# Four transformer layers on one core: VectorE makes the softmax levels of the quantised layer, and its feed-forward is laid over three phases

## The reference

```python
def _fq(x, delta, zp, n_bits):
    xi = _round_ste(x / delta) + zp
    xq = jnp.clip(xi, 0.0, 2.0 ** n_bits - 1.0)
    return (xq - zp) * delta

def _attn(x, ctx, wq, wk, wv, wo, bo, dq, dk, dv, dw):
    ...
    sim = jnp.einsum('bhid,bhjd->bhij', _fq(q, dq, 128.0, 8), _fq(k, dk, 128.0, 8)) * SCALE
    attn = jax.nn.softmax(sim, axis=-1)
    out = jnp.einsum('bhij,bhjd->bhid', _fq(attn, dw, 0.0, 8), _fq(v, dv, 128.0, 8))
    ...
h1 = _ln(x, ln1_g, ln1_b)
x = _attn(h1, h1, a1_wq, ...) + x
h2 = _ln(x, ln2_g, ln2_b)
x = _attn(h2, context, a2_wq, ...) + x
h3 = _ln(x, ln3_g, ln3_b)
hg = h3 @ ff_w1 + ff_b1
a, g = jnp.split(hg, 2, axis=-1)
x = a * jax.nn.gelu(g, approximate=False) @ ff_w2 + ff_b2 + x
```

## Time and profile before

| | us |
|---|---|
| median of 3 runs (range) | 2011.68 (2011.1 to 2012.37) |
| the profiled execution | 2007.97 |
| its span in the trace | 2006.2 |
| layer 1, from the first score of its first phase to the end of its last full phase | 631.76 |
| PE / DVE / ACT / POOL busy in the whole span | 1808.6 / 1237.6 / 1074.7 / 905.3 |
| PE / DVE / ACT / POOL busy in those 631.76 | 553.14 / 337.72 / 386.03 / 311.02 |

### The profile page before, as it was taken

The page is one execution under the profiler, slowest core; times in us unless marked ns, Lnnn a source line. Parts: engine busy times, 40 slices in busy tenths (PEclk is TensorE's granted clock), DMA queues, the critical chain, the costliest instruction groups (busy, mean ns, idle before and its releaser), DMA issues.

```text
span 2006.2 us, 34807 instructions
## 1 busy us (share of the span) xinstructions
PE 1808.6 (90%) x12481; PEld 1344.1 (67%) x12481; DVE 1237.6 (62%) x2220; ACT 1074.7 (54%) x3142; POOL 905.3 (45%) x1209
## 2 busy tenths in 40 slices
PE   4998988789799889889999999999999999999997
PEld 4887876466566656657667677676676676766766
DVE  5899995744654464463575665865746647365471
ACT  2232225665575475565575564655645656565662
POOL 4466554654463363363254443644444333333340
PEclk8999998788878878879999999999999999999999
DMA  7200000002000000000002000000000000000000
GB/s 226 92 11 6 11 6 6 1 7 90 1 6 6 1 6 6 0 6 7 1 7 90 1 7 6 7 7 1 7 6 2 12 1 7 22 7 1 12 1 11
DMA packets 31073, 35.66 MB, mean 18 GB/s; under 512 B 3164, under 2 KB 29752, under 8 KB 30520
## 3 DMA queue, kind: packets, MB, share of 16 engines
q1 hardware_dynamic: 30904, 33.44, 5.2%
HBM read 31.34 MB, written 2.10 MB: 17 GB/s over the span
## 4 chain that ended last, share of the span: by engine, by line
PE 61%; DVE 17%; ACT 10%; issue 6%; POOL 2%; SPq 2%; DMA 1%; DVEq 0%; POOLq 0%; ACTq 0%
PE ps L594 33%; PE ps L806 6%; PE ps L744 6%; PE ps L816 5%; PE ps L850 4%; ACT work L983 3%; ACT work L990 3%; DVE work L1183 3%; DVE xn L1037 2%; PE ps L607 2%; DVE rowmax L1187 2%; PE ps L831 2%; ACT hT L899 1%; PE ps L766 1%; POOL work L1376 1%
## 5 line engine op out<-in xcount | busy, mean ns | idle before, releaser
L594 PE MATMUL ps<-hT,w_slot 128*128 128x256 f32 x1696 | 410.1, 396 | 17.1 <-ACT hT L899 16.1
L1300 POOL TENSOR_TENSOR work<-KT,own_head 128x512 f32<-128x512 f32 x256 | 262.4, 1046 | 285.4 <-PE ps L806 179.9
L594 PEld LDWEIGHTS ps<-hT,w_slot 128*128 128x128 f32 x1696 | 323.5, 196 | 77.2 <-ACT hT L899 21.7
L990 ACT ACTIVATE work<-work,rowmax 128x128 f32<-128x128 f32 x768 | 244.9, 391 | 167.8 <-DVE rowmax L1187 167.0
L816 PEld LDWEIGHTS ps<-ident,work 128*128 128x128 f32 x1536 | 200.1, 153 | 170.0 <-issue 90.4
L983 ACT ACTIVATE work<-ps,rowmax,score_scale 128x128 f32<-128x128 f32 x512 | 229.3, 484 | 118.7 <-DVE rowmax L1191 118.3
L816 PE MATMUL ps<-ident,work 128*128 128x128 f32 x1536 | 266.4, 302 | 17.9 <-ACT work L990 17.0
L806 PE MATMUL ps<-work,QT 128*128 128x512 f32 x512 | 266.4, 605 | 10.0 <-POOL work L1300 4.9
L1376 POOL TENSOR_SCALAR work<-work,winv 128x128 f32<-128x128 f32 x512 | 185.0, 382 | 167.7 <-DVE winv L1203 165.3
L1217 DVE RECIPROCAL O<-ps 128x128 f32<-128x128 f32 x128 | 122.3, 955 | 174.6 <-PE ps L850 173.9
L976 ACT ACTIVATE work<-ps 128x512 f32<-128x512 f32 x256 | 150.7, 596 | 91.4 <-PE ps L816 91.2
(11 more groups left out here) (131 smaller groups left out, 3170.3 us busy)
## 6 DMA issues: line engine op xcount, KB each, us to landing
ctx_in<-in_ctx SPq DMA_DIRECT2D x32, 256.0 KB, 2.7
w_slot<-in_L_xattn_W SPq DMA_DIRECT2D x2, 1024.0 KB, 6.2
w_slot<-in_L_xattn_ff_w SPq DMA_DIRECT2D x1, 2048.0 KB, 11.5
w_slot<-in_L_xattn_ffn_w SPq DMA_DIRECT2D x2, 1024.0 KB, 9.8
w_slot<-in_L_xattn_w SPq DMA_DIRECT2D x2, 1024.0 KB, 10.0
out<-x_all SPq DMA_DIRECT2D x8, 256.0 KB, 2.1
x_all<-in_x SPq DMA_DIRECT2D x1, 1536.0 KB, 11.4
pad<-in_mask_Bx1x1xS_fk SPq DMA_DIRECT2D x1, 1024.0 KB, 7.6
```

The source lines that it names most:

```text
L594: mm = pe.matmul(dst, lhsT(k), rhs(k), start=(k == 0 and not onto), stop=(k == chunks - 1 and not more))
L990: ex = act.activation(prob[i % NPF][:, tok(h)], src[:, tok(h)], ACT.Exp, bias=shifts[:, at:at + 1])
L1300: pool.tensor_tensor(KB[u % NK].rearrange("p (h k) -> p h k", h=HU), keys, own_head[:, e:HC:2].unsqueeze(2).broadcast_to([P, HU, S]), ALU. ...
```

## The change

Two things are changed in layer 1, and the order of its pieces.

1. **Levels.** ScalarE's line 974 and the constants `top` and `below` are gone. VectorE takes a turned unit out of PSUM with the smaller of x and MAGIC + 255, minus MAGIC: the level itself. Its place in VectorE's queue is behind the row maximum and the inverses of the same step. Line 831 multiplies only the levels, four matmuls for a unit, and the output scale loses its minus sign.
2. **Order.** For the groups 0 to 2 the feed-forward of a stream is cut in three: four `f` in steps 8 to 11 of one phase, four in steps 8 to 11 of the next, and `y2` in four parts in steps 0 to 3 of the one after that. Stream 0 has its first four `f` in C, its last four in D and its `y2` in the next A; stream 1 has them in the next A, B and C. So every one of these phases carries four `f`, and A and C also a `y2`. The chain that ends in `k`, `q`, `v` of the next group goes along in C and D. Group 3, which leads into layer 2, keeps `joined` for its own feed-forward.
3. **Banks.** In these phases the feed-forward has bank `one` alone: every `f` writes it, and waits until VectorE has read the one before. `ctx`, `tin`, `k`, `q`, `v` and `y` share `other`; so `q` waits for `k_ready` and `v` for `q_ready`.

```diff
+SPREAD_START = {"tin": 3, "ctx": 4, "bias": 4, "k": 7, "q": 8, "v": 9, "keys": 9}
+SPREAD_NORM = {"norm": 8, "scale": 10}
+SPREAD_HIDDEN = 8
+SPREAD_SUM = 4
...
+    hidden = [(SPREAD_HIDDEN + int(piece[1:]) % (FC // 2), piece, arg, n) for piece, _, arg, n in pieces[:y2] if piece[0] == "f"]
+    product = [(part, f"y2{part}", pieces[y2][2], pieces[y2][3]) for part in range(Y2)]
...
+                attend(layer, g, 1, 0, middle(0) + into_a)
...
+                attend(layer, g, 0, 1, middle(1) + start(0, SPREAD_NORM) + into_b)
+                chain_0, first_0, second_0, product_0 = end(0)
+                attend(layer, g, 1, 1, chain_0 + start(0, SPREAD_START) + first_0 + start(1, SPREAD_NORM) + into_c)
+                chain_1, first_1, second_1, product_1 = end(1)
+                attend(*after, 0, 0, chain_1 + start(1, SPREAD_START) + second_0)
+                return product_0 + first_1, second_1, product_1
...
+                            pe.wait_ge(q["k_ready" if piece == "q" else "q_ready"], C * (use("att", layer, g, n["att"]) + 1))
...
+                            pe.wait_ge(q["hid_ready"], FC * use("ffn", layer, g, n["ffn"]) + f)
+                        product(one[:, 0:T], lambda k: w1[:, k, FF + f * P:FF + (f + 1) * P], lambda k: hT[st][:, k, :], C)
...
-                            rhs = below[:, :].broadcast_to([P, S]) if n < 2 else PTb[u % 2][:, tok(2 * x + e)]
...
-                            act.activation(PTb[u % 2], bank(2 + u % 2), ACT.Relu, bias=top[:, 0:1], scale=-1.0).then_inc(s["PT_ready"], 1)
...
+                def levels(u):
+                    dve.wait_ge(s["o_ps"], U * ap + u + 1 - 2)
+                    dve.wait_ge(s["PT_ps"], U * ap + u + 1)
+                    dve.tensor_scalar(PTb[u % 2], bank(2 + u % 2), MAGIC + 255.0, MAGIC, ALU.min, ALU.subtract).then_inc(s["PT_ready"], 1)
```

More of the change, by code:

```diff
@@ L172, with spread_closing @@
 FIRST_AHEAD = 2
+SPREAD = 1
+MIDDLE_SHIFT = {"yadd": -1}
+SPREAD_START = {"tin": 3, "ctx": 4, "bias": 4, "k": 7, "q": 8, "v": 9, "keys": 9}
+SPREAD_NORM = {"norm": 8, "scale": 10}
+SPREAD_CLOSING = {"ot": 0, "y": 1, "sum": 1, "norm": 2, "scale": 4, "tin": 6, "bias": 8}
+SPREAD_HIDDEN = 8
+SPREAD_SUM = 4
+def spread_closing(layer):
+    pieces = PLAN[layer][-1]
+    y2 = [piece for piece, _, _, _ in pieces].index("y2")
+    chain = [(SPREAD_CLOSING[piece], piece, arg, n) for piece, _, arg, n in pieces[:y2] if piece[0] != "f"]
+    hidden = [(SPREAD_HIDDEN + int(piece[1:]) % (FC // 2), piece, arg, n) for piece, _, arg, n in pieces[:y2] if piece[0] == "f"]
+    product = [(part, f"y2{part}", pieces[y2][2], pieces[y2][3]) for part in range(Y2)]
+    product.append((SPREAD_SUM,) + pieces[y2 + 1][0:1] + pieces[y2 + 1][2:])
+    return chain, hidden[:FC // 2], hidden[FC // 2:], product
 CLOSING_SLOT = {"ot": 0, "y": 1, "sum": 1, "norm": 2, "scale": 3, "post": 5, "tin": 7, "bias": 8}
@@ L476, in passes @@
             left = []
[L477 to L481, removed]
+            for g in range(NG - 1):
+                left = joined_pass(0, g, (0, g + 1), left)
+            before_last(0)
+            left = joined_pass(0, NG - 1, (1, 0), left), [], []
+            for g in range(NG - 1):
+                left = spread_pass(SPREAD, g, (SPREAD, g + 1), left)
+            before_last(SPREAD)
+            left = spread_pass(SPREAD, NG - 1, (SPREAD + 1, 0), left)
             for layer in range(FIRST_AHEAD, NL):
@@ L882, in emit @@
                         act.wait_ge(q["ctx_ps"], use("ctx", layer, g, 0) + 1)
-                        act.activation(cT[st].rearrange("p c t -> p (c t)"), one, ACT.Copy).then_inc(q["ctx_ready"], 1)
+                        act.activation(cT[st].rearrange("p c t -> p (c t)"), other if spread else one, ACT.Copy).then_inc(q["ctx_ready"], 1)
                     elif piece == "stage":
@@ L896, in emit @@
                         act.wait_ge(q["tin_ps"], due("tin", layer, g, n["tin"]) + 1)
+                        target = hT_ahead[st] if ahead and not (spread and n["att"] == PER_PASS["att"][layer]) else hT[st]
                         for m in range(C):
@@ L934, in emit @@
                         k = use("ffn", layer, g, n["ffn"])
-                        b = one if f % 2 == 0 else other
+                        b = one if spread or f % 2 == 0 else other
                         if arg["act"] == "geglu":
@@ L1013, in emit @@
                 def emit(piece, arg, n):
+                    spread = ahead == "spread"
                     swapped = ahead or "early" in arg
@@ L1018, in emit @@
                         if n["yadd"]:
-                            dve.wait_ge(q["yadd_done"], G * use("yadd", layer, g, n["yadd"]))
+                            dve.wait_ge(q["yadd_done"], G * due("yadd", layer, g, n["yadd"]))
                         else:
@@ L1225, in step @@
                         inverses((i - SUM_LAG) // 2)
+                    if quant and 0 <= i - lag < U:
+                        levels(i - lag)
                     u = i - lag - 1
```

90 lines of the change are left out of this document (71 added, 19 removed).

## The result

The changed kernel takes 2030.38 us (median of 4 runs, 2028.32 to 2030.99), the kernel before 2011.39 beside it: a ratio of 1.0099, 95% interval 1.0085 to 1.0113. The forecast was 1975, with 2024 as the upper end. It is slower, and outside the range. Times are medians; one run of e12 took 6116.01 us, and is in that kernel's median but not in its ratio.

The account below looks back on a forecast made before the run. TensorE, 90% busy, has an idle first half in A and B and a packed second in C and D; evening out takes a group from 160.6 to 149.6. Summed over the layer, 2011.68 - 36.9 = 1975 us; range 1938 to 2024.

Parts of the forecast that it names:

- The phases that keep their order ... lose `below` only.: First phase, A and B of group 0, C of group 3: -0.7 us each, -2.8 in all.
- I let it return in the same place: TensorE's clock returns to full within a few us of the start of `k`, as before the change.
- rival 2: Clock stays low in second halves: +8.9 us a phase, range 2020 to 2082, value 2040; chance 0.12.
- The Trainium skill's rule: Short idles between groups of matmuls make the clock go up and down; speaks against the change, toward the second rival's sum.
- First half with `y2`: A and C up to `k`: 19.0 us, 2.5 more than 16.5, for 7.07 of `y2` work.
- `tin` and `ctx`, 0.7 us: Two more transposed pieces in C and D push ScalarE: C 39.0 against A 38.3, D 36.5 against B 35.8.
- Levels, a gain of 0.5 in the first half: Levels take 0.75 us on VectorE; without the product with `below`, first half goes from 17.0 to 16.5.
- Quantising 1.8 and 2.25: Second half of a spread phase: VectorE needs 1.8 us for quantised `k`, 2.25 each for `q` and `v`.
- rival 3: VectorE's queue becomes the bound: 4.25 us by 12 phases, +51, 2026; chance 0.12.
- The second half, 15.9: Spread phase from `k`'s end to next first score: 15.9 us, TensorE waiting 1.85; a phase B had 7.9.
- The sum over the layer: Layer 1: D -46.7, C -35.8, A and B +45.9, last `y2` +2.5, phases keeping order -2.8: -36.9 us.
- make the 8.0: Second half's growth from 7.9 to 15.9: four `f` 7.1, waits 1.85, 0.7 less for `below`.

Follow-up runs that it names:

- e12: The kernel before with the four transposes of units 0 to 3 issued twice in each phase: 1998.17 us, ratio 0.9944.
- e3: The changed kernel with `q` in the feed-forward's idle bank again in phases A and B of group 0: 2016.36 us, ratio 1.0025.
- e5: The changed kernel with the four transposes of units 0 to 3 issued twice in each phase: 1993.90 us, ratio 0.9922.
- e8: The kernel before with the levels of units 0 to 3 on VectorE and those of units 4 to 7 on ScalarE: 1998.97 us, ratio 0.9947.
- e1: The kernel before with all levels on VectorE and no products with the constant, old order and banks: 2016.51 us, ratio 1.0026.
- e6: The changed kernel without the second of three quantising instructions (clip at 127 and rounding) for `q`, `k`, `v`: 1999.60 us, ratio 0.9944.
- e15: The changed kernel with `q` in the idle bank in A0 and B0, levels split between VectorE and ScalarE, transposes of units 0 to 3 twice: 1989.34 us.
- e14: The kernel before with levels split between VectorE and ScalarE and transposes of units 0 to 3 issued twice: 1982.95 us, ratio 0.9866.
- e20: The changed kernel with GpSimd's keys for the next phase waiting for the quantised `v` instead of `k`: 2014.69 us, ratio 1.0025.
- e13: The changed kernel with `q` in the idle bank in A0 and B0 and transposes of units 0 to 3 twice: 1989.92 us, ratio 0.9908.
- e2: The changed kernel with levels back on ScalarE and constant products back on TensorE, leaving new order and banks: 2017.52 us, ratio 1.0030.
- e4: The changed kernel with the four feed-forward products of phases B and D at steps 4 to 7 instead of 8 to 11: 2046.21 us, ratio 1.0174.

## Why the prediction was wrong

By its own steps:
- *"The phases that keep their order ... lose `below` only."* This failed most clearly. A and B of group 0 keep their pieces but not their banks: `q` and `v` wait in the open. Forecast 29.9 and 26.6, measured 37.6 and 32.7, 13.8 too long. e3 shows the cause (8.0 of it, and 5.4 more in C0 and D0); the levels behind `q` and `v` are a second one there.
- *"I let it return in the same place"*, of the clock. Right in A2, where `q` ran at full clock; wrong in C0, D0, C1 and C2, where `q` was at half clock (3.78 for 1.8); C2 took 44.4 for 39.0, about 2 us of it by this and most of the rest in its first half. That rival 2 wanted waits of 0.35 to 1.15 us to keep the clock down in every phase is not what happened either. e5 and e12: cheap work against the low level gives 36 us in the changed kernel and 11 in the one before. The Trainium skill's rule, weighed in the prediction, pointed the right way, to a clock that costs the new order more, here by 25 us; but its short idles alone do not keep the clock low, for in e5 they are longer (1.36 and 1.18) and `k` and `q` take 1.99.
- *First half with `y2`, 2.5 us.* Mis-sized: A2 stands 3.7 us above B2 up to `k` (20.6 and 16.9), C2 3.8 above D2 (22.4 and 18.5), and C3 went from 16.6 to 22.9.
- *`tin` and `ctx`, 0.7 us.* Mis-sized: D2 is 1.6 above B2 up to `k`. These two terms are 1.2 by 5, 3.8 for C3 and 0.9 by 6: 15 us of the 55 by which the phases are over.
- *Levels, a gain of 0.5 in the first half.* They took 0.68, just under the 0.70 to 0.77 that were named, and first halves were shorter (e8: 16.3 for 17.0 in B2). What the forecast left out is their place in the second half (e1: 1.55 more in B2, 1.1 in A2).
- *Quantising 1.8 and 2.25.* Right in most phases; 2.29 and 3.26 for one instruction in A0 and D0 were in neither the forecast nor rival 3, though the earlier trace rows held the small case.
- *The second half, 15.9.* Right where the clock came back: 16.2 in A2, 16.3 in B2, with 1.18 and 0.9 for `k` and 0.43 to 0.6 for `hid`.
- *The sum over the layer.* A was entered three times at +7.8, but A1 had been 27.57 and not 30.49 before. By its own phase times the forecast adds up to 34.6 us less, not 36.9: 1977. And the terms behind *"make the 8.0"* make 8.25. Neither slip matters beside the 55.

Of the rivals the third, VectorE's queue, is nearest in its time (2026) and in part in its place: e6 gained 31 us from one instruction less of VectorE's quantising. The second, the clock, has the result inside its range of 2020 to 2082, and held for one product in four of the twelve phases.

Why is the new order no gain even where all this is mended? e15 has the forecast's phases nearly as written: D 36.8, A 38.7, B 36.2, C 41.0, in all 152.6 for 149.6. But the old order with the same two edits is at 154.1 (e14), not at 160.6. More than half of the 11 us forecast for a group was the clock and the levels, which the old order can have too; spreading the feed-forward by itself moves four products of 1.9 us from one full stretch into another. Over the layer it is 3.1 us behind e14; C3 alone is 6.5 longer.

Open: how the 36 us of e5, the 14 of e3 and the 16 of e20 divide. They overlap (e13 gives 40 for 50), since a wait, a low clock and a meeting with GpSimd bring each other about: in each of the three kernels the 3.26 us of D0 are gone. Why `q` of D0 is at one level in one kernel and at the other in the next, behind the same wait, is open too.

## What to carry to other kernels

When a change makes two users share a buffer, walk every phase in which either appears, above all those with nothing to cover the new wait. A forecast that moves work out of a stretch at low clock must price what the clock does to both kernels: here cheap extra work for TensorE in its idle steps was worth more (11 to 36 us) than the rearrangement. Give both kernels that work before judging an order: here it took the whole loss away. Before an engine takes over work, look at what stands ahead of it in its queue at each place, not at its busy share.

## What the runs showed of the hardware

- Four transposes repeated for 64 units, 256 of a kernel's 12,000 matmuls, made it 36 us quicker: with them the mean granted clock of the layer is 0.92 instead of 0.83.
- Behind a `k` of 3.78 us and a wait of 0.66, the same product took 3.77 us in one kernel and 1.99 in two others; and twelve runs of one kernel (e2) fell into two bunches some 10 us apart, with a mean granted clock of about 0.946 and 0.940.
- An SBUF to SBUF instruction on VectorE that takes 0.43 us took 3.26 beside three of GpSimd's in a row.
- A change between Gelu and Exp on ScalarE is a load of 1.283 us each time; layer 1 of e4 has 62 loads. The Trainium skill, page "ScalarE: Activation LUTs", section "What ACT_TABLE_LOAD costs", gives the same figure for the load, and the trace agrees. The page adds a drain of about 1.38 us to every switch; the trace does not show it: where its input is there, the next instruction starts 0.01 us behind the load.
